# The order of scores and values inside each burst of split-array matmuls

## The chip, the cores and the metric

One core of one Trainium2 chip runs the whole kernel. The metric is the device time of one execution in microseconds (us); the time before is a median of three runs.

## The reference, cut to what matters

```python
def attention(x, context):            # x: 64 x 128 x 256, context: 64 x 128 x 192
    q = (x @ w_q)                      # 16 heads of 64
    k = (context @ w_k)
    v = (context @ w_v)
    attn = softmax(q @ k.T * 64 ** -0.5)
    return (attn @ v) @ w_o + b_o

x = x + attention(layernorm(x), ctx)
h = layernorm(x)
gates = softmax(h @ gate), top 2 of 8 experts, divided by their sum
x = x + sum(gate_e * (relu(h @ W1_e + b1_e) @ W2_e + b2_e))
```

Everything is float32. The kernel keeps the precision of the large products by splitting an operand in a high and a low part (`_h`, `_l`) and adding three products.

## The kernel before, in words

The 8192 tokens are taken as 32 pairs of sequences. The first stage (attention and routing) is one pipeline over the pairs, `iterations`: iteration -1 to 31 and an epilogue, of which 2 to 30 are one hardware loop. The second stage runs tiles of 256 tokens through the experts and is not touched by the change.

Each engine has its own program with the same eight steps n = 0 to 7 in an iteration, written out by hand; the engines meet at semaphores. One iteration handles eight units of attention, u0 to u7. A unit is four heads of one sequence: one bank of scores, 128 queries by 4 x 128 keys.

The steps of TensorE (`body` in the tensor block) are these.

- `scores(it, n)`, at even n, makes the scores of the units n and n+1 at once. A head has 64 channels, so that two heads stand in the two row halves of the array: 8 matmuls of 64 rows and 128 columns, which write `bank_s0` and `bank_s1` in turn (L1422). It may write only when ScalarE has read both banks of the units before: it waits for `s_exp` of unit n-1.
- `transposes` turns the probabilities of the unit two steps before (`LATE`) into `bank_t` (L1411), after GpSimd has normalised them (`s_norm`).
- `product` makes one of the projections that `A_SLOTS` lists for the step: q and k (L1404, L1471, L1472), v (L1479, L1480, L1404), the output o (`three` at L1404), the transposed input t (L1453) and the routing f0.
- `values(it, name, n)`, at the end of odd n, multiplies v with the transposed probabilities of two units: 8 matmuls with all 128 rows and 64 columns, in the two column halves of the array, into `bank_v` (L1437). `VALUES` names them: w3 of the pair before at n = 1, w0, w1 and w2 at n = 3, 5 and 7. It waits for `t_copy` (the transposed probabilities are in SBUF), for `v_lo` (`bank_v` is read out) and for the v product.

So `values` of an odd step and `scores` of the next even step stand next to each other, four times in an iteration. I call the two together a burst, and name it by its even step; 8 matmuls are 16 records in the trace.

The other engines do this with it. VectorE takes the lowest score (`lowest`, L951) when a bank is full. ScalarE takes the exponentials with it (`exps`, L777, four heads, with a record of READ_ACCUMULATOR behind each), copies the transposed probabilities (`copy_t`, L770), the q, k and t products (`hi_part`, L787 to L792) and the context (L828), and reads `bank_v` first (`hi_out`, L807). VectorE reads `bank_v` behind it (`low_out`, L1004), copies v (L969), subtracts the high part of the context (L1157) and makes the routing. GpSimd normalises (`norm`, L669) and sends rows by an indirect DMA (`send`, L662). Every engine works its own list strictly in the order written; ScalarE's list has `hi_out` at the end of an odd step, before `copy_t` and `exps` of the next even step.

The waits at the head of the two functions, and the last lines of `body`:

```python
def scores(it, n):
    ...
    wait(pe, a_hi, it if g else it - 1, "q11" if g else "k01")
    wait(pe, s_exp, it, f"u{n + 1}", 2)
...
def values(it, name, n):
    ...
    wait(pe, a_done, it if name == "w2" else it - 1, f"v{g}{b}")
    wait(pe, t_copy, it, LATE[n][0])
    wait(pe, v_lo, it, LAST[n - 1][0])
...
        if n in VALUES and has(it, VALUES[n][1]):
            values(it, VALUES[n][0], n)
```

Of the kernel before, what the change touches and what calls it, by code (L numbers as in the profile page):

```python
# [62 lines left out]
def wait(engine, signal, it, name, back=0):  # L63

    value = signal.at(it, name)
    if isinstance(value, int):
        value -= back
        if value > 0:
            engine.wait_ge(signal.sem, value)
    else:  # L70
        engine.wait_ge(signal.sem, value - back)


def program(nc, x, ctx, w_all, w_ot, b_o, b_oc, gate, gate_t, w12, b1, b2, out):
# [5 lines left out]
    PAIRS = tokens // (2 * P)  # L80
# [68 lines left out]
    VALUES = {1: ("w3", PREV), 3: ("w0", CUR), 5: ("w1", CUR), 7: ("w2", CUR)}  # L149
# [3 lines left out]
    with ex:  # L153
        def sem(name):
            return ex.enter_context(nc.semaphore(name))
# [29 lines left out]
        made = sem("made")  # L185
        with ExitStack() as a:
# [165 lines left out]
            def has(it, of):  # L352
                first, last = {PREV: (1, PAIRS), CUR: (0, PAIRS - 1), NEXT: (-1, PAIRS - 2), BOTH: (-1, PAIRS),
                               FROM0: (0, PAIRS)}[of]
                return not isinstance(it, int) or first <= it <= last
# [1044 lines left out]
            def _(pe):  # L1400
# [6 lines left out]
                def transposes(it, name, n):  # L1407
                    wait(pe, s_norm, it - 1 if n >= 6 else it, name)
                    wait(pe, t_copy, it, name, 1)
                    for h in range(4):  # L1410
                        last = pe.transpose(bank_t[:, h * P:(h + 1) * P], prob[:, n % 4, h, :], ident[:, :])  # L1411
                    last.then_inc(t_full.sem, 1)

                def scores(it, n):

                    g, b = n // 4, (n % 4) // 2
                    wait(pe, a_hi, it if g else it - 1, "q11" if g else "k01")
                    wait(pe, s_exp, it, f"u{n + 1}", 2)
                    for c in range(CHUNKS // 2):
                        for side in range(2):  # L1420
                            part = slice(side * HEAD, (side + 1) * HEAD)
                            last = pe.matmul(bank_s[side][:, c * P:(c + 1) * P], qt[part, g, c, b * P:(b + 1) * P],  # L1422
                                             kt[part, g, b, c, :], start=True, stop=True, skip_group_check=True)
                            if c == CHUNKS // 2 - 1:
                                last.then_inc(s_full.sem, 1)

                def values(it, name, n):
                    g, b = int(name[1]) // 2, int(name[1]) % 2
# [5 lines that stand above are left out]
                    for head in range(HALF):  # L1434
                        unit, h = head % 2, head // 2
                        side = slice(unit * HEAD, (unit + 1) * HEAD)
                        last = pe.matmul(bank_v[side, h * P:(h + 1) * P],  # L1437
                                         vv[:, g, b, head * HEAD:(head + 1) * HEAD], probt[:, unit, h, :],
                                         start=True, stop=True, skip_group_check=True)
                    last.then_inc(v_full.sem, 1)  # L1440
# [95 lines left out]
                def body(it):  # L1536
                    for n in range(8):

                        if isinstance(it, int) and it == -1 and n == 5:
                            pe.wait_ge(w_lo, Q_READY)  # L1540
                        if isinstance(it, int) and it == 1 and n == 0:
                            pe.wait_ge(w_lo, NW)
                            pe.wait_ge(gate_made, 5)
                        late, of = LATE[n]
                        if n % 2 == 0 and has(it, CUR):
                            scores(it, n)
                        if has(it, of):
                            transposes(it, late, (n - 2) % 8)
                        slots = A_SLOTS_LAST if isinstance(it, int) and it == PAIRS - 1 else A_SLOTS
                        for name, o in slots[n]:  # L1550
                            if has(it, o):
                                if isinstance(it, int) and it == -1 and name == "k00":
                                    pe.wait_ge(w_lo, K_READY)
                                if isinstance(it, int) and it == -1 and name == "v00":
                                    pe.wait_ge(w_lo, V_READY)
                                product(it, name)
                                if isinstance(it, int) and it == -1 and name == "t0":
                                    bias_scores()
                                    keep_busy(8)
                        if n in VALUES and has(it, VALUES[n][1]):  # L1560
                            values(it, VALUES[n][0], n)

                def keep_busy(many):

                    for _ in range(many):
                        pe.matmul(bank_s[0][:, 0:P], prob[:, 0, 0, :], prob[:, 0, 0, :], start=True, stop=True,
                                  skip_group_check=True)
# [10 lines left out]
                def bias_scores():  # L1578

                    pe.wait_ge(gate_made, 2)  # L1580
                    for c in range(DC):
                        last = pe.matmul(bank_v[:, E:2 * E], bo_col[:, c:c + 1].to_broadcast([P, P]), gate_c[:, c, :],
                                         start=c == 0, stop=c == DC - 1, skip_group_check=True)
                    last.then_inc(gate_mean, 1)

                gate_means()
                keep_busy(3)
                pe.wait_ge(made, 20)
                iterations(pe, body)

                def turn_x(j, u):
# [116 lines left out]
```

## Time and profile before

| | |
|---|---|
| median of 3 runs | 1581.21 us (1580.75 to 1581.81) |
| the profiled execution, its own time | 1580.22 us |
| its span in the trace | 1578.5 us |
| TensorE, matmul | 1553.8 us busy, 98% |
| TensorE, weight loads | 1454.0 us busy, 92% |
| VectorE | 1176.1 us busy, 75% |
| ScalarE | 1108.0 us busy, 70% |
| GpSimd | 818.1 us busy, 52% |
| mean granted TensorE clock | 0.994 of full speed |

The profiled execution takes 1.7 us more than its span, which lies around the traced instructions, and is 1.0 us below the median. In the stretch from 95 to 1109 us, which is the looped part of the first stage, TensorE is busy 1011.46 of 1014 us at granted clock 1.00. The busy share counts a matmul from its start to its modelled end, and matmuls overlap; how long a piece of work holds the engine is read from the starts of it and of what follows.

### The profile page before, as it was taken

Reading aid. Unit: us, or ns where it says so; the run is one execution under the profiler, and the core shown is the slowest. Engines: PE = TensorE matmul, PEld = TensorE weight load, DVE = VectorE, ACT = ScalarE, POOL = GpSimd, SP = SyncE. Lnnn points to the kernel's source line nnn. Section 1 sums busy time; section 2 is a strip of 40 time slices with the busy share of each in tenths; the row PEclk is TensorE's granted clock in tenths of the full one; section 3 lists DMA queues with packets and bytes.
Section 4 is the critical chain, followed back from the end, with each engine's and each line's share of the span. In section 5 each row is a group of like instructions: output and inputs, shape, how many; then the busy total and the mean of one; then the engine's idle time right before and its main releaser. Section 6 shows DMA issues by size and latency. Waiting matters only on the chain.

```text
span 1578.5 us, 45424 instructions
## 1 busy us (share of the span) xinstructions
PE 1553.8 (98%) x14150; PEld 1454.0 (92%) x14151; DVE 1176.1 (75%) x3796; ACT 1108.0 (70%) x3357; POOL 818.1 (52%) x946
## 2 busy tenths in 40 slices
PE   8999999999999999999999999999999999999997
PEld 7899999999899999999999989998899999999997
DVE  4777777777777777777777777777788777777775
ACT  5677677677776777767767777676666676777774
POOL 2344545545554554554555455455456555555556
PEclk9999999999999999999999999999999999999999
DMA  6522111222111221211122211122799755555554
GB/s 201 145 72 74 60 60 60 77 90 72 62 60 60 67 94 66 74 60 60 63 75 89 74 60 60 60 67 81 241 231 249 144 86 85 89 86 90 84 84 61
DMA packets 105643, 145.05 MB, mean 92 GB/s; under 512 B 12736, under 2 KB 87616, under 8 KB 105344
## 3 DMA queue, kind: packets, MB, share of 16 engines
q1 hardware_dynamic: 60144, 89.00, 17.8%
q0 software_dynamic: 26816, 37.32, 13.7%
q10 hardware_dynamic: 18640, 18.19, 4.4%
q8 instruction: 23, 0.38, 0.1%
q14 instruction: 20, 0.16, 0.0%
HBM read 77.09 MB, written 67.38 MB: 92 GB/s over the span
## 4 chain that ended last, share of the span: by engine, by line
issue 47%; POOL 22%; PE 9%; DVE 7%; DMA 6%; DVEq 3%; ACT 2%; POOLq 2%; ACTq 1%; SPq 0%
POOL lists L662 7%; DMA out<-stage_room,number 6%; PE bank_a L1404 4%; POOL prob L669 3%; DVE hid L1332 3%; POOL rstd L648 2%; DVE stage_room L1349 2%; POOL stage_room L711 2%; POOL stage_room L707 2%; POOL out L735 2%; DVEq L1344 1%; PE bank_v L1437 1%; POOLq L729 1%; PE bank_s L1422 1%; DVEq L1323 1%
## 5 line engine op out<-in xcount | busy, mean ns | idle before, releaser
L669 POOL TENSOR_TENSOR prob<-prob,inv 128x512 f32<-128x512 f32 x256 | 271.4, 1060 | 520.3 <-DVE inv L956 519.6
L777 ACT ACTIVATE prob<-bank_s,low 128x128 f32<-128x128 f32 x1024 | 363.3, 376 | 40.9 <-DVE low L951 40.9
L735 POOL DMA_INDIRECT out<-stage_room,number x142 | 231.8, 1632 | 53.9 <-issue 53.1
L951 DVE TENSOR_REDUCE low<-bank_s 128x4 f32<-128x512 f32 x256 | 175.4, 685 | 98.0 <-PE bank_s L1422 97.9
L777 ACT ACTIVATION_READ_ACCUMULATOR prob<-bank_s,low 128x1 f32 x1024 | 221.1, 216 | 0.0
L770 ACT ACTIVATE probt<-bank_t 128x512 f32<-128x512 f32 x256 | 153.4, 599 | 89.6 <-PE bank_t L1411 89.6
L1050 DVE SCALAR_TENSOR_TENSOR stage_room<-xin,wo_t 128x256 f32<-128x256 f32 x480 | 178.8, 426 | 0.0
L807 ACT ACTIVATE ot_h<-bank_v 128x512 fp32r<-128x512 f32 x128 | 77.4, 604 | 138.4 <-PE bank_v L1437 138.4
L885 ACT ACTIVATE hidt_h<-hid 128x512 fp32r<-128x512 f32 x142 | 89.7, 632 | 117.4 <-DVE hid L1332 112.2
L1411 PE MATMUL bank_t<-ident,prob 128*128 128x128 f32 x1024 | 161.9, 281 | 4.0 <-POOL prob L669 4.0
L1404 PE MATMUL bank_a<-xt_l,wq_h 128*128 128x256 f32 x512 | 152.4, 298 | 0.3 <-DVE xt_l L966 0.3
L1422 PE MATMUL bank_s<-kt,qt 64*128 64x128 f32 x2048 | 149.7, 286 | 2.3 <-ACT prob L777 2.3
L1422 PEld LDWEIGHTS bank_s<-kt,qt 64*128 64x128 f32 x2048 | 125.1, 188 | 24.6 <-issue 24.4
L662 POOL DMA_INDIRECT lists<-rows,slot x128 | 129.0, 1008 | 33.8 <-issue 33.8
L1404 PE MATMUL bank_a<-wo_l,ot_h 128*128 128x264 f32 x496 | 146.1, 295 | 0.0
L1404 PE MATMUL bank_a<-xt_h,wq_h 128*128 128x256 f32 x512 | 144.5, 282 | 0.0
L1404 PE MATMUL bank_a<-xt_h,wq_l 128*128 128x256 f32 x512 | 144.4, 282 | 0.0
L865 ACT ACTIVATE wst<-homes 128x2048 fp32r x71 | 136.2, 1918 | 9.2 <-issue 9.0
L1437 PE MATMUL bank_v<-probt,vv 128*64 128x128 f32 x2048 | 140.9, 280 | 0.7 <-DVE ot_l L1004 0.4
L1404 PE MATMUL bank_a<-wo_h,ot_l 128*128 128x264 f32 x496 | 141.0, 284 | 0.0
L1404 PE MATMUL bank_a<-wo_h,ot_h 128*128 128x264 f32 x496 | 140.7, 284 | 0.0
L1411 PEld LDWEIGHTS bank_t<-ident,prob 128*128 128x128 f32 x1024 | 114.1, 141 | 25.3 <-POOL prob L669 5.9
(231 smaller groups left out, 4728.9 us busy)
## 6 DMA issues: line engine op xcount, KB each, us to landing
stage_room<-lists ACTq DMA_DIRECT2D x67, 265.0 KB
halves<-stage_room SPq DMA_DIRECT2D x32, 512.0 KB
homes<-halves SPq DMA_DIRECT2D x16, 1024.0 KB, 6.4
xin<-in_x SPq DMA_DIRECT2D x32, 256.0 KB, 2.8
stage_room<-in_x SPq DMA_DIRECT2D x32, 256.0 KB
stage_room<-in_w SPq DMA_DIRECT2D x32, 256.0 KB, 4.3
out<-stage_room SPq DMA_DIRECT2D x32, 256.0 KB, 2.2
cin<-in_ctx SPq DMA_DIRECT2D x32, 128.0 KB, 2.6
```

Of the source, the lines that this page charges most:

```text
L662: pool.indirect_dma_start(lists, bass.IndirectOffsetOnAxis(ap=slot[:, b, k:k + 1], axis=0), rows[:, b, :], None).then_inc(sent, 16)
L669: pool.tensor_tensor(prob[:, n % 4, :, :], prob[:, n % 4, :, :], wide(inv[:, n % 4, :], P), ALU.mult).then_inc(s_norm.sem, 1)
L735: pool.indirect_dma_start(out, bass.IndirectOffsetOnAxis(ap=number[:, u, b:b + 1], axis=0), ysum[:, u, b, :], None, compute_op=ALU.add).th ...
L770: act.activation(probt[:, n % 2, :, :], bank_t[:, :].rearrange("p (h q) -> p h q", h=4), ACT.Copy).then_inc(t_copy.sem, 1)
L777: e = act.activation(prob[:, n % 4, h, :], bank_s[n % 2][:, h * P:(h + 1) * P], ACT.Exp, bias=low[:, n % 4, h:h + 1], scale=-1.0, accum_ou ...
L865: act.activation(wst[u % 2][:, :, :, :], homes[:, bass.ds(e, 2 * DC * H)].rearrange("p (c s h) -> p c s h", c=DC, s=2), ACT.Copy)
L951: dve.tensor_reduce(low[:, n % 4, :], bank_s[n % 2][:, :].rearrange("p (h k) -> p h k", h=4), AX.X, ALU.min).then_inc(s_low.sem, 1)
L1050: last = dve.scalar_tensor_tensor(junk[:, k % 11, :], xin[:, b, :], 1.0, gate_b[:, e, :], ALU.mult, ALU.mult, accum_out=x_two[:, b, e:e + 1])
L1404: last = pe.matmul(dst, stat[s], move[r], start=start and m == 0, stop=stop and m == 2)
L1411: last = pe.transpose(bank_t[:, h * P:(h + 1) * P], prob[:, n % 4, h, :], ident[:, :])
L1422: last = pe.matmul(bank_s[side][:, c * P:(c + 1) * P], qt[part, g, c, b * P:(b + 1) * P], kt[part, g, b, c, :], start=True, stop=True, ski ...
L1437: last = pe.matmul(bank_v[side, h * P:(h + 1) * P], vv[:, g, b, head * HEAD:(head + 1) * HEAD], probt[:, unit, h, :], start=True, stop=Tru ...
```

## The change

`values` is no longer called at the end of its odd step, but in the even step behind it, after that step's `scores` and before its `transposes`; at n = 0 it is the w2 of the iteration before. Only at the end of the last iteration is w2 still called in its own step, since no scores follow there. Nothing else moves, on no engine.

```diff
@@ -1544,6 +1544,11 @@
                         late, of = LATE[n]
                         if n % 2 == 0 and has(it, CUR):
                             scores(it, n)
+                        if (n - 1) % 8 in VALUES:
+                            name, made = VALUES[(n - 1) % 8]
+                            values_of = it - 1 if n == 0 else it
+                            if has(values_of, made):
+                                values(values_of, name, (n - 1) % 8)
                         if has(it, of):
                             transposes(it, late, (n - 2) % 8)
                         slots = A_SLOTS_LAST if isinstance(it, int) and it == PAIRS - 1 else A_SLOTS
@@ -1557,7 +1562,7 @@
                                 if isinstance(it, int) and it == -1 and name == "t0":
                                     bias_scores()
                                     keep_busy(8)
-                        if n in VALUES and has(it, VALUES[n][1]):
+                        if isinstance(it, int) and (it, n) == (PAIRS - 1, 7):
                             values(it, VALUES[n][0], n)
```

TensorE's list in the hardware loop at burst 6, before. `bank_v` is written by the values (`probt` are the transposed probabilities, `vv` is v), `bank_s` by the scores; a row of REGISTER_ALU is the sequencer's arithmetic for a semaphore value.

```order
L1404 MATMUL bank_a<-xt_h,wk_h 128x256
L71 REGISTER_ALU [waits t_copy,a_done]
L1437 MATMUL bank_v<-probt,vv 64x128 [waits v_lo]
L1437 MATMUL bank_v<-probt,vv 64x128 x7
L1422 MATMUL bank_s<-kt,qt 128x128 [waits s_exp,a_hi]
L1422 MATMUL bank_s<-kt,qt 128x128 x7
L1411 MATMUL bank_t<-ident,prob 128x128 [waits t_copy,s_norm]
L1411 MATMUL bank_t<-ident,prob 128x128 x3
```

The same place in the changed kernel:

```order
L1404 MATMUL bank_a<-xt_h,wk_h 128x256
L1422 MATMUL bank_s<-kt,qt 128x128 [waits s_exp,a_hi]
L1422 MATMUL bank_s<-kt,qt 128x128 x7
L71 REGISTER_ALU [waits t_copy,a_done]
L1437 MATMUL bank_v<-probt,vv 64x128 [waits v_lo]
L1437 MATMUL bank_v<-probt,vv 64x128 x7
L1411 MATMUL bank_t<-ident,prob 128x128 [waits t_copy,s_norm]
L1411 MATMUL bank_t<-ident,prob 128x128 x3
```

The wait for `s_exp` now stands ahead of both groups, where only the scores were behind it before; the transposes are behind both groups in either order.

At the top of the loop, burst 0, the values stood at the end of the loop's body, before its branch, and the list began with the scores:

```order
L348 ISA
L71 REGISTER_ALU [waits a_hi]
L1422 MATMUL bank_s<-kt,qt 128x128 [waits s_exp]
L1422 MATMUL bank_s<-kt,qt 128x128 x7
L71 ISA
L71 REGISTER_ALU [waits s_norm]
L1411 MATMUL bank_t<-ident,prob 128x128 [waits t_copy]
```

and now the values follow them there:

```order
L348 ISA
L71 REGISTER_ALU [waits a_hi]
L1422 MATMUL bank_s<-kt,qt 128x128 [waits s_exp]
L1422 MATMUL bank_s<-kt,qt 128x128 x7
L71 ISA
L71 REGISTER_ALU [waits a_done]
L71 ISA [waits t_copy]
L1437 MATMUL bank_v<-probt,vv 64x128 [waits v_lo]
L1437 MATMUL bank_v<-probt,vv 64x128 x7
L71 REGISTER_ALU [waits s_norm]
L1411 MATMUL bank_t<-ident,prob 128x128 [waits t_copy]
```

The values have crossed the loop's branch, and one more row of the sequencer stands in the burst.

## Rows read from the trace of the kernel before

**Rows 1.** Busy time by stretch, the looped part (PE, PEld, DVE, ACT, POOL, clock)

```profile
95.00:1109.00 1014.00, 1011.46 (x9603) 922.86 (x9603) 764.53 (x2770) 724.51 (x2639) 522.41 (x651) 1.00 0.21 69
```

**Rows 2.** Timeline of PE, one loop iteration's bursts 0, 2 and 6 (start, us, instruction)

```profile
500.69 1.09 PE L1437 MATMUL bank_v<-probt,vv 128*64 128x128 f32 x16
...
509.38 1.09 PE L1437 MATMUL bank_v<-probt,vv 128*64 128x128 f32 x16
...
523.19 0.40 PE L1404 MATMUL bank_a<-wv_h,xt_h 128*128 128x512 f32 x1
...
526.58 1.09 PE L1437 MATMUL bank_v<-probt,vv 128*64 128x128 f32 x16
527.60 1.16 PE L1422 MATMUL bank_s<-kt,qt 64*128 64x128 f32 x16
528.69 0.66 PE L1411 MATMUL bank_t<-ident,prob 128*128 128x128 f32 x4
...
534.53 0.39 PE L1404 MATMUL bank_a<-wv_h,xt_h 128*128 128x512 f32 x1
534.85 1.09 PE L1437 MATMUL bank_v<-probt,vv 128*64 128x128 f32 x16
```

**Rows 3.** Timeline of ACT, the same iteration

```profile
501.83 0.60 ACT L807 ACTIVATE ot_h<-bank_v 128x512 fp32r<-128x512 f32 x1 [1.19 <-PE bank_v L1437]
...
508.39 0.23 ACT L777 ACTIVATION_READ_ACCUMULATOR prob<-bank_s,low 128x1 f32 x1
...
523.70 0.63 ACT L828 ACTIVATE xt_h<-cin 128x512 fp32r<-128x512 f32 x1 [0.40 <-PE bank_a L1404]
...
525.70 0.37 ACT L777 ACTIVATE prob<-bank_s,low 128x128 f32<-128x128 f32 x1 [0.87 <-DVE low L951]
...
526.99 0.21 ACT L777 ACTIVATION_READ_ACCUMULATOR prob<-bank_s,low 128x1 f32 x1
...
529.38 0.60 ACT L770 ACTIVATE probt<-bank_t 128x512 f32<-128x512 f32 x1 [0.20 <-PE bank_t L1411]
...
534.53 0.27 ACT L777 ACTIVATION_READ_ACCUMULATOR prob<-bank_s,low 128x1 f32 x1
```

**Rows 4.** Timeline of DVE, the same iteration

```profile
523.62 0.69 DVE L969 COPY vv<-bank_a 128x512 f32<-128x512 f32 x1 [0.23 <-PE bank_a L1404]
...
524.98 0.68 DVE L951 TENSOR_REDUCE low<-bank_s 128x4 f32<-128x512 f32 x1
```

**Rows 5.** Timeline of PE, scores that had no values ahead (iteration 0)

```profile
22.09 0.39 PE L1404 MATMUL bank_a<-wv_h,xt_h 128*128 128x512 f32 x1
22.41 1.16 PE L1422 MATMUL bank_s<-kt,qt 64*128 64x128 f32 x16
...
28.57 1.16 PE L1422 MATMUL bank_s<-kt,qt 64*128 64x128 f32 x16 [2.18 <-ACT prob L777]
```

**Rows 6.** Timeline of ACT, what those scores waited for

```profile
28.21 0.22 ACT L777 ACTIVATION_READ_ACCUMULATOR prob<-bank_s,low 128x1 f32 x1
```

**Rows 7.** Instructions of bank_s: durations in ns, min/median/max

```profile
L1422 PE MATMUL bank_s<-kt,qt x2048: 272/272/580, 22.4 to 1108.0; 64*128 64x128 f32 x187
```

**Rows 8.** Timeline of PE, values that had no scores behind (epilogue)

```profile
1120.56 1.09 PE L1437 MATMUL bank_v<-probt,vv 128*64 128x128 f32 x16 [0.36 <-issue]
1121.59 0.66 PE L1607 MATMUL bank_a<-ident,stage_room 128*128 128x128 f32 x4
```

**Rows 9.** Timelines of PE and of ACT, burst 6 of iteration 30

```profile
1073.99 1.09 PE L1437 MATMUL bank_v<-probt,vv 128*64 128x128 f32 x16
...
1074.41 0.21 ACT L777 ACTIVATION_READ_ACCUMULATOR prob<-bank_s,low 128x1 f32 x1
```

**Rows 10.** Timeline of PE, transposes that waited (iteration 31)

```profile
1104.14 0.66 PE L1411 MATMUL bank_t<-ident,prob 128*128 128x128 f32 x4 [1.73 <-POOL prob L669]
```

**Rows 11.** Timelines of ACT and of POOL around burst 4 of the same iteration

```profile
518.90 0.98 POOL L662 DMA_INDIRECT lists<-rows,slot  x1 [0.30 <-issue]
...
520.51 0.60 ACT L807 ACTIVATE ot_h<-bank_v 128x512 fp32r<-128x512 f32 x1 [1.30 <-PE bank_v L1437]
```

## The prediction

> **What bounds the kernel.** I read the busy time by stretch first. In the looped part of the first stage TensorE is busy 1011.46 of 1014 us at granted clock 1.00, VectorE 764, ScalarE 725, GpSimd 522 [rows 1]: TensorE sets the pace, and only its own list can change the time. Next I read TensorE's timeline over one iteration. Burst 0 begins at 500.69 and again at 534.85 [rows 2]: 34.16 us for an iteration, with no wait for another engine in it. So the question is what the swap does to (a) the time that a burst holds TensorE and (b) the waits at its head. For (b) I read, at each burst, when ScalarE finished the exponentials that the scores wait for.
>
> **(a) The switches of the array.** The matmuls are the same, and so are their number and sizes; what changes is who stands next to whom.
> Product to values takes 0.32 us from start to start (534.53 to 534.85) [rows 2]; product to scores, in iteration 0 with no values ahead, also 0.32 (22.09 to 22.41) [rows 5].
> Values to scores takes 1.02 (526.58 to 527.60) [rows 2]; values to transposes, in the epilogue, 1.03 (1120.56 to 1121.59) [rows 8].
> Scores to transposes takes 1.09 (527.60 to 528.69) [rows 2].
> Two of the three new neighbours are therefore in the trace, at the old price. Scores to values is not. The nearest row is scores to transposes, 1.09, which also goes from row halves to all rows, and I take that: a burst costs 0.32 + 1.09 + 1.02 in either order, a difference of 0.
> The bounds: a record of the scores lasts 0.272 [rows 7], so 16 of them that span 1.16 start every (1.16 - 0.27) / 15 = 0.059 us, the last at 0.89, and 0.20 passes from it to the next instruction. If that switch cost nothing, it would be 0.14 less; if it cost one such loss more, 0.14 more. There are 126 bursts with both parts (2 in iteration 0, 4 in each of 1 to 31), so this term lies between -18 and +18 us.
> No row shows this switch, and there the Trainium skill has a rule, in TensorEngine Tiling (Array Packing), Key Properties: a change of tiling mode drains the engine. A burst has three such changes in both orders, so by that page too the term is 0.
> The further row of the sequencer in burst 0 I cost at nothing: such rows stand in front of the scores there already, and TensorE has a matmul in flight over them. The branch is now between a product and the scores; between values and scores it lost nothing visible.
>
> **(b) The waits at the head of a burst.** The scores of burst n may start once the exponentials of unit n-1 are done. Behind the last exponential's record there is a hand-over: in iteration 0 the record ended at 28.43 [rows 6] and the scores that waited for it started at 28.57 [rows 5], 0.14 later.
> Burst 6: the values start at 526.58 [rows 2], but the exponentials of u5 end at 526.99 + 0.21 = 527.20 [rows 3]. Until now the values ran under that and the scores at 527.60 found all ready. Now the scores come first and cannot start before 527.34: **a wait of 0.76 us.**
> Do these exponentials come earlier in the changed kernel? They start at 525.70 after ScalarE sat idle 0.87 for the lowest scores of u5 [rows 3]. VectorE makes those from 524.98, behind the copy of v at 523.62, for which it sat idle 0.23 until TensorE's product [rows 4], whose last matmul started at 523.19 [rows 2]. From 523.62 on VectorE's three instructions are back to back. The chain is hung on a product of TensorE that keeps its distance from burst 6, and the scores of burst 4, though 1.02 earlier, don't shorten it. I take the wait whole.
> It is so in every iteration from 0 to 28 and in 30: there the values start at 1073.99 and the record ends at 1074.62 [rows 9], 0.63 later, as at 526.58 and 527.20 (in the first two within 0.1 of it). In 29 GpSimd was late with the transposes just before, and the exponentials were done in time. 30 x 0.76 = 22.8.
> Burst 0: the exponentials of u7 end at 534.53 + 0.27 = 534.80 [rows 3] and the burst begins at 534.85 [rows 2], so the scores would wait until 534.94: 0.09. ScalarE is busy without a gap from its copy at 529.38 [rows 3], which comes after the transposes of burst 6; the wait there moves both by the same amount, so the 0.09 stays. 30 such bursts (iterations 2 to 31): 2.7.
> Burst 2: the exponentials are done at 508.39 + 0.23 = 508.62 [rows 3] and the burst begins at 509.38 [rows 2], 0.76 later and more than 0.14; burst 4 is alike. Nothing.
> In the last iteration the transposes of u3 wait 1.73 for GpSimd [rows 10], behind scores that now come 1.02 earlier; but the scores of burst 6, which wait there already, now hold the values and transposes back by about 1.0. I take 0, between -1 and +1.
>
> That the wait costs all of its length rests on TensorE's list being worked in order. The row shows it: scores that waited 2.18 in iteration 0 left the engine idle, with transposes and products behind them [rows 5]. The Trainium skill says the same in TensorE: Matmul & The Clock Gate, on which tiles overlap: weight loads may be pulled ahead, matmuls start and end in strict order. By the page the sum is mine; if the values, ready all the time, could pass the waiting scores, their 1.02 would cover the 0.76 and the sum would be about 0.
>
> **What moves and costs nothing.** The lowest scores can be taken 1.02 earlier at each burst, which gives VectorE and GpSimd slack that TensorE doesn't wait for. `bank_v` is full 1.09 later. ScalarE reads it 1.14 after the values start (501.83) [rows 3], now at 500.69 + 1.09 + 1.14 = 502.92, and is done at 503.5. ScalarE's idle time (1.19 at this read) ahead of this read covers the shift; if it were gone, the copy of the transposed probabilities would be late, and the exponentials after it. No DMA and no queue is passed by anything moved.
>
> **The sum.** 0 + 22.8 + 2.7 = +25.5 us. The profiled execution took 1580.22, so 1605.7 for it; it lies 1.0 below the median, and the median should become **1606.7 us**. An iteration should take 34.16 + 0.85 = 35.0. A measurement of this kernel can tell about 0.2% (3.2 us) from no change.
>
> **The rivals.**
> *Not slower.* The burst's own time shrinks by more than the waits: the scores' successor costs less when it is the values. Per iteration 0.85 of waits has to be won in 4 bursts, 0.21 each; that is the point from which it decides. The 0.14 lost after the scores isn't enough (25.5 - 18 = +7.5, 1589); with a third of the entry's 0.32 (0.10) won too it would be 25.5 - 126 x 0.24 = -4.7, 1576.5. For it: the one switch that no row shows. Against: the entry and the exit are in the trace, at the old price. 4% for faster, 4% for about no change; in the latter I also put that TensorE passes the waiting scores by (1581).
> *The switch costs more.* Another 0.14 at each of 126 bursts: +18, 1624. 5%.
> *ScalarE slips at burst 4.* There it reads `bank_v` at 520.51 [rows 11], not 1.14 after the values' start at 518.50 but 0.87 later, in each of the iterations 2 to 28 and 30, those in which GpSimd's last indirect DMA starts at 518.90 [rows 11]. If that delay is tied to the DMA's time, it is over when the read is now due (518.50 + 1.09 + 1.14 = 520.73), and nothing happens. If it goes with the read, that comes at 521.60, 1.09 late; some 0.20 of idle time before the copy (as at 529.38) and 0.40 before the context's copy [rows 3] take 0.60 of it, and 0.49 reaches the exponentials of u5 and the wait at burst 6: 28 x 0.49 = +14, 1620. The same distance to the DMA in all these iterations speaks for the first. 13%.
> *The wait at burst 6 is shorter,* since VectorE runs ahead somewhere that I don't see: half of it gives 1595. 6%.
>
> **How the numbers follow.** The forecast, 1606.7, has 68%, with a few us either way for the hand-over and the last iteration. The range takes in the forecast with a mixture of the halved wait or a cheaper switch below, and the slip above: 1597 to 1620; outside lie the cases of no loss and the dearer switch. Faster 4%, same 4%, slower 92%.
>
> **What would show it.** In the changed profile the scores should wait for ScalarE's exponentials some 60 times, 30 of them about 0.7 us, at burst 6 and burst 0 only; an iteration should be 35.0 us; scores to values should be 1.09 and values to transposes 1.03; ScalarE's wait for `bank_v` should grow and VectorE's for `bank_s` fall. I am wrong on (a) if the distance from scores to values isn't 1.09, and on (b) if the exponentials of u5 end earlier against the last matmul of the product of v than the 4.01 us of here (from 523.19 to 527.20).

## The result, and the profile after

The changed kernel takes **1604.05 us** (median of 4 runs, 1602.72 to 1605.78), the kernel before 1581.51 on the same chip (4 runs, 1580.75 to 1581.89). The ratio is 1.0142, 95% interval 1.0127 to 1.0157: slower by 22.5 us. Forecast were 1606.7 and +25.5. The profiled execution of after took 1605.78 (span 1604.0), 25.6 more than the profiled one of before.

TensorE's share of the span falls from 98 to 97%. Its busy time grows from 1553.8 to 1557.5 us, so that 21.8 of the 25.5 us by which the span grew are idle time. The page of after, in its part on busy time, in the group of the scores (after "|" busy time and mean ns; then the idle time before them and what ended most of it), and in the chain:

```profile
PE 1557.5 (97%) x14150; PEld 1457.4 (91%) x14151; DVE 1175.8 (73%) x3796; ACT 1105.0 (69%) x3357; POOL 809.2 (50%) x946
...
PE 83%; ACT 4%; DVE 4%; issue 3%; DMA 2%; POOL 1%; DVEq 1%; ACTq 0%; SPq 0%; POOLq 0%
...
L1422 PE MATMUL bank_s<-kt,qt 64*128 64x128 f32 x2048 | 148.7, 284 | 24.7 <-ACT prob L777 24.6
```

The list of waits of after (total us, times, longest). The last line is the new one:

```profile
ACT ot_h L807 <- PE bank_v L1437: 245.9, 127, 3.2
...
DVE low L951 <- PE bank_s L1422: 37.2, 65, 3.5
ACT prob L777 <- DVE low L951: 33.6, 34, 4.4
...
PE bank_s L1422 <- ACT prob L777: 24.6, 32, 2.2
```

The same lines of before: 

```profile
ACT ot_h L807 <- PE bank_v L1437: 138.4, 95, 2.4
DVE low L951 <- PE bank_s L1422: 97.9, 126, 4.1
ACT prob L777 <- DVE low L951: 40.9, 65, 4.4
...
PE bank_s L1422 <- ACT prob L777: 2.3, 2, 2.2
```

TensorE waited 2.3 us for exponentials before and waits 24.6 now, in 32 places instead of 2. ScalarE waits longer for `bank_v`, which is full later; VectorE waits less for `bank_s`, which is full earlier. Both signs are as forecast.

Where those waits stand shows in TensorE's timeline of after, over one iteration (bursts 6 and 0, then 4, for [rows 2]):

```profile
502.64 0.39 PE L1404 MATMUL bank_a<-wv_h,xt_h 128*128 128x512 f32 x1
...
505.81 0.28 PE L1404 MATMUL bank_a<-xt_h,wk_h 128*128 128x256 f32 x1
506.79 1.16 PE L1422 MATMUL bank_s<-kt,qt 64*128 64x128 f32 x16 [0.70 <-ACT prob L777]
507.88 1.09 PE L1437 MATMUL bank_v<-probt,vv 128*64 128x128 f32 x16
508.91 0.66 PE L1411 MATMUL bank_t<-ident,prob 128*128 128x128 f32 x4
...
514.75 0.39 PE L1404 MATMUL bank_a<-wv_h,xt_h 128*128 128x512 f32 x1
515.07 1.16 PE L1422 MATMUL bank_s<-kt,qt 64*128 64x128 f32 x16
516.16 1.09 PE L1437 MATMUL bank_v<-probt,vv 128*64 128x128 f32 x16
517.19 0.66 PE L1411 MATMUL bank_t<-ident,prob 128*128 128x128 f32 x4
...
532.88 1.16 PE L1422 MATMUL bank_s<-kt,qt 64*128 64x128 f32 x16
533.98 1.09 PE L1437 MATMUL bank_v<-probt,vv 128*64 128x128 f32 x16
```

Only burst 6 waits, 0.70 us; its scores are 0.77 late, since the last product's modelled end reaches 0.07 further into the wait, and these 0.07 count as busy. Burst 0 starts 0.32 after the last product's start, without a wait. Scores to values is 1.09 and values to transposes 1.03. The next burst 0 begins at 550.00: an iteration takes 34.93 us, not 34.16.

ScalarE's timeline of after at the same two places (for [rows 3]):

```profile
505.14 0.37 ACT L777 ACTIVATE prob<-bank_s,low 128x128 f32<-128x128 f32 x1 [0.87 <-DVE low L951]
...
506.44 0.21 ACT L777 ACTIVATION_READ_ACCUMULATOR prob<-bank_s,low 128x1 f32 x1
...
514.75 0.27 ACT L777 ACTIVATION_READ_ACCUMULATOR prob<-bank_s,low 128x1 f32 x1
```

The exponentials of u5 end at 506.44 + 0.21 = 506.65 and the scores that waited start at 506.79, 0.14 later, the hand-over of [rows 5, 6]. ScalarE has waited 0.87 for the lowest scores, exactly as before [rows 3], and from the last matmul of the product of v (502.64) to the end of the exponentials are 4.01 us, as many as before: the chain did not move against TensorE's products.

### The profile page after: what moved, and what is told of

It is laid out like the page before. It is cut to its first block, busy times and chain, and to the rows that moved or that the text cites. A ratio compares the mean times of both kernels' runs of the same rounds, so it can differ in the third digit from the quotient of the medians.

```text
span 1604.0 us, 45424 instructions
## 1 busy us (share of the span) xinstructions
PE 1557.5 (97%) x14150; PEld 1457.4 (91%) x14151; DVE 1175.8 (73%) x3796; ACT 1105.0 (69%) x3357; POOL 809.2 (50%) x946
## 4 chain that ended last, share of the span: by engine, by line
PE 83%; ACT 4%; DVE 4%; issue 3%; DMA 2%; POOL 1%; DVEq 1%; ACTq 0%; SPq 0%; POOLq 0%
PE bank_a L1404 35%; PE bank_s L1422 9%; PE bank_v L1437 8%; PE bank_t L1411 7%; PE bank_t L1404 5%; PE bank_v L1404 5%; PE bank_s L1404 5%; ACT prob L777 2%; PE bank_a L1479 2%; PE bank_a L1480 2%; PE bank_a L1471 1%; PE bank_a L1472 1%; PE bank_a L1612 1%; DMA out<-stage_room,number 1%; DVE low L951 1%
## 5 line engine op out<-in xcount | busy, mean ns | idle before, releaser
L777 ACT ACTIVATE prob<-bank_s,low 128x128 f32<-128x128 f32 x1024 | 363.3, 378 | 33.6 <-DVE low L951 33.6
L1050 DVE SCALAR_TENSOR_TENSOR stage_room<-xin,wo_t 128x256 f32<-128x256 f32 x480 | 174.4, 418 | 0.0
L1422 PE MATMUL bank_s<-kt,qt 64*128 64x128 f32 x2048 | 148.7, 284 | 24.7 <-ACT prob L777 24.6
```

The costliest lines, as they stand in the source:

```text
L777: e = act.activation(prob[:, n % 4, h, :], bank_s[n % 2][:, h * P:(h + 1) * P], ACT.Exp, bias=low[:, n % 4, h:h + 1], scale=-1.0, accum_ou ...
L1050: last = dve.scalar_tensor_tensor(junk[:, k % 11, :], xin[:, b, :], 1.0, gate_b[:, e, :], ALU.mult, ALU.mult, accum_out=x_two[:, b, e:e + 1])
```

## The experiments

The theory was that the whole loss is one wait per iteration, of burst 6 for the exponentials of u5, and that the new neighbours on the array cost nothing. The rivals were a dearer or cheaper switch, paid at all bursts, and a slip of ScalarE. All kernels below compute everything that the reference does. Ratios are taken against the kernel before on the same chip: 1580.63 (27 runs, 1578.27 to 1582.58) for e1 to e4, and 1579.37 (17 runs, 1577.16 to 1582.4) for e5 to e7.

### One burst of four, and the other three

In `e1_burst6_only` the scores go first at burst 6 alone; `e2_bursts_0_2_4` is its complement. Against the changed kernel (of e2 the set is `(0, 2, 4)` in both lines):

```diff
-                        if (n - 1) % 8 in VALUES:
+                        if (n - 1) % 8 in VALUES and n in (6,):
...
-                        if isinstance(it, int) and (it, n) == (PAIRS - 1, 7):
+                        own = (n + 1) % 8 not in (6,) or (isinstance(it, int) and (it, n) == (PAIRS - 1, 7))
+                        if n in VALUES and has(it, VALUES[n][1]) and own:
```

> Scores first at burst 6 alone; bursts 0, 2 and 4 as in the kernel before. Theory A (the loss is the wait of the scores of burst 6 for the exponentials of u5, the order itself costs nothing): 0.77 us in each of iterations 0 to 30, some 1604, and TensorE's wait for ScalarE's exponentials about 0.70 us, 29 to 31 times. Rival B (scores to values is a dearer switch and costs its share at each burst): a quarter of the loss, some 1587. Rival C (the later reading of bank_v at bursts 0, 2 and 4 holds back ScalarE): the wait would be shorter here than in the changed kernel and the time below 1600. Beside it: ScalarE's reading of bank_v at burst 4 should again be late, about 2.0 us after the start of the values instead of 1.14, in iterations 2 to 30; if so, an exponential of u4 and all behind it are as before.

> Scores first at bursts 0, 2 and 4, values first at burst 6. Theory A: no wait for exponentials in the loop, 34.16 us for an iteration, 1581 to 1583 in all; what is left is iteration 0, where ScalarE reads bank_v 1 us later in front of the copy of w_o, and the transposes of u3 wait 1 us or more longer for GpSimd. Rival B (dearer switch): three quarters of the loss, some 1598. The hand-over at burst 0 that the prediction put at 0.09 us each should not show: at most 0.03.

e1: 1602.94 us (4 runs, 1601.81 to 1604.63), ratio 1.0141 [1.0126, 1.0157]: the whole loss, from a quarter of the edit. e2: 1582.31 (11 runs, 1580.26 to 1583.5), ratio 1.0011 [1.0001, 1.0020], within what I called no change: three quarters of the edit, 94 of the 126 new neighbours, cost at most 3.2 us. In the lists of waits, first of e1, then of e2:

```profile
PE bank_s L1422 <- ACT prob L777: 23.6, 31, 2.2
```

```profile
PE bank_s L1422 <- ACT prob L777: 2.5, 2, 2.2
```

An iteration of e1 takes 34.93 us, one of e2 34.16. A switch priced at 126 bursts is out, in either direction, and so is a wait at burst 0: e2 has scores first there, and none waits.

### The exponentials made earlier

If burst 6 waits because u5's exponentials are late, VectorE can mend it: `e3_after_early_lowest` is the changed kernel with the lowest scores of u5 taken behind the copy of `v10`, ahead of the context's low part and the copy of `v11` (not in the last iteration). `e4_before_early_lowest` makes the same edit in the kernel before, as a control.

```diff
-                        if has(it, CUR):
+                        last = isinstance(it, int) and it == PAIRS - 1
+                        if has(it, CUR) and (n != 5 or last):
                             lowest(it, n)
...
                         for name, of in slots[n][1:]:
-                            outcome(it, made_in, name, of)
+                            if name != "v11" or last:
+                                outcome(it, made_in, name, of)
+                        if n == 4 and has(it, CUR) and not last:
+                            lowest(it, 5)
...
+                        if n == 4 and not last:
+                            outcome(it, made_in, "v11", CUR)
```

> The changed kernel, with the lowest scores of u5 taken by VectorE right behind the copy of the v product v10, in front of the context's low part and of the copy of v11 (which it now follows). Theory A: the exponentials of u5 start at ScalarE's own pace behind its copy, about 0.9 us earlier against the product of v11, and end 0.2 us before burst 6: the wait of 0.70 goes away entirely, 34.16 us for an iteration, 1581 to 1584 in all. If the chain behind the wait is another one (ScalarE's copies rather than VectorE's list), the wait stays at 0.4 or more and the time above 1594. Rival B: no change against the changed kernel, 1604.

> The kernel before with the same move on VectorE's list as in the run above, and values first everywhere. Control: no wait of TensorE is taken away by it, so 1581.5 within 1.5 us. If it were faster, a gain in the run above would not belong to the wait alone; if it were slower, the low part of the context or the copy of v11 holds TensorE, at the k product of step 5 or at the values.

e3: 1582.52 us (11 runs, 1579.84 to 1584.43), ratio 1.0010 [1.0001, 1.0019]: the changed order, at all four bursts, without its loss. e4: 1580.93 (11 runs), ratio 1.0001 [0.9992, 1.0010]: the edit by itself gives nothing. The list of waits of e3 (lines moved by 6: L1428 are the scores):

```profile
ACT prob L777 <- DVE low L951: 6.7, 3, 4.4
PE bank_s L1428 <- ACT prob L777: 3.7, 2, 2.2
```

ScalarE's wait for the lowest scores went from 33.6 us in 34 places to 6.7 in 3, and TensorE's from 24.6 to 3.7. An iteration takes 34.16 again. The wait at burst 6 is the loss, all but 1.9 us of it; the order as such, at 126 bursts, costs no more than that.

### The rest of 1.7 to 1.9 us: iteration 0

e2 and e3 have no wait at burst 6 and are still 1.7 and 1.9 above the kernel before. Their traces differ from it in iteration 0, where `prepare` makes `w_o`'s high part on ScalarE (L765) and low part on VectorE (L941) behind the read of `bank_v` at burst 4. `e5_024_not_first` is e2 with that one burst in the old order:

```diff
-                        if (n - 1) % 8 in VALUES and n in (0, 2, 4):
+                        if (n - 1) % 8 in VALUES and n in (0, 2, 4) and not (isinstance(it, int) and (it, n) == (0, 4)):
...
-                        own = (n + 1) % 8 not in (0, 2, 4) or (isinstance(it, int) and (it, n) == (PAIRS - 1, 7))
+                        own = (n + 1) % 8 not in (0, 2, 4) or (isinstance(it, int) and (it, n) in ((PAIRS - 1, 7), (0, 3)))
```

> Scores first at bursts 0, 2 and 4, values first at burst 6 and at burst 4 of iteration 0. The theory on what remained of the loss (1.7 us with bursts 0, 2 and 4, 1.9 us with the early lowest scores): in iteration 0 ScalarE reads bank_v ahead of its copy of w_o, which the scores' reduction on VectorE waits for, so that scores first at this one burst costs 1.1 us. Then the wait of the transposes of u3 in iteration 0 goes from 2.96 back to 1.9 or less, and the time to 1580.6 to 1581.6. Rival: the remainder lies in the last iteration, or is not there; then that wait is shorter and the time stays 1.7 above the kernel before.

1579.13 us (12 runs, 1576.1 to 1580.93), ratio 0.9997 [0.9989, 1.0006]: no rest is left to be seen. TensorE's timeline of e5, the transposes of u3 in iteration 0; in after they wait 2.96 there, before 0.45:

```profile
46.57 0.65 PE L1411 MATMUL bank_t<-ident,prob 128*128 128x128 f32 x4 [1.18 <-POOL prob L669]
```

Iteration 0 is also where TensorE's clock differs from one execution to the next, so single waits there are rough. That the order matters there rests on the medians of e2 and e5, each against its own kernel before: +1.7 and -0.2. These intervals overlap a little, so the term, 1.9 us by the medians, is barely clear of the noise, and its size is not well known.

### What a change of the array's division costs

The prediction had no row for a division change by itself. `e6_before_halves` cuts each burst of the kernel before into half of the values, half of the scores, and the other halves: the same matmuls, two more changes per burst.

```diff
                         if n % 2 == 0 and has(it, CUR):
-                            scores(it, n)
+                            before_it = it - 1 if n == 0 else it
+                            name, made = VALUES[(n - 1) % 8]
+                            if has(before_it, made):
+                                scores(it, n, (0, 1))
+                                values(before_it, name, (n - 1) % 8, range(4, 8))
+                                scores(it, n, (2, 3))
+                            else:
+                                scores(it, n)
...
                         if n in VALUES and has(it, VALUES[n][1]):
-                            values(it, VALUES[n][0], n)
+                            alone = isinstance(it, int) and (it, n) == (PAIRS - 1, 7)
+                            values(it, VALUES[n][0], n, range(8) if alone else range(4))
```

> The order before, with each burst cut in four: half of the values, half of the scores, the other half of the values, the other half of the scores. The matmuls are the same; a burst has two changes of the array's division more. By the rows of the kernel before (0.20 us from the last scores to what follows, 0.22 from the last values, against 0.055 inside) each costs about 0.15: 126 bursts x 0.30 = 38, with some 0.2 us of wait at burst 6 about 1622. Rival: the 0.15 is lost only when the work that follows is of all rows and all columns, and a change between the two divisions is cheap: below 1600.

1631.14 us (4 runs, 1628.65 to 1633.01), ratio 1.0320 [1.0305, 1.0335]: +51.8. TensorE's timeline of e6, a burst 2 and the burst 6 of one iteration:

```profile
535.66 0.66 PE L1437 MATMUL bank_v<-probt,vv 128*64 128x128 f32 x8
536.25 0.72 PE L1423 MATMUL bank_s<-kt,qt 64*128 64x128 f32 x8
536.89 0.66 PE L1437 MATMUL bank_v<-probt,vv 128*64 128x128 f32 x8
537.48 0.71 PE L1423 MATMUL bank_s<-kt,qt 64*128 64x128 f32 x8
538.13 0.66 PE L1411 MATMUL bank_t<-ident,prob 128*128 128x128 f32 x4
...
553.57 0.66 PE L1437 MATMUL bank_v<-probt,vv 128*64 128x128 f32 x8
554.34 0.71 PE L1423 MATMUL bank_s<-kt,qt 64*128 64x128 f32 x8
554.99 0.66 PE L1437 MATMUL bank_v<-probt,vv 128*64 128x128 f32 x8
555.57 0.71 PE L1423 MATMUL bank_s<-kt,qt 64*128 64x128 f32 x8
556.22 0.66 PE L1411 MATMUL bank_t<-ident,prob 128*128 128x128 f32 x4
```

Eight values take 0.59 to the scores where sixteen take 1.02 [rows 2]: a matmul is (1.02 - 0.59) / 8 = 0.054, and 0.59 - 8 x 0.054 = 0.16 is the change. Eight scores take 0.64 to the values where sixteen take 1.09: 0.056 each, and 0.19 for the change. The plain burst lasts 2.47 instead of 2.11 from its first values to the transposes. The second burst lasts 2.65: with half of the values the scores start only 0.59 behind, and u5's exponentials aren't done, so they start 0.18 later still. 96 x 0.36 + 30 x 0.54 = 50.8 of the 51.8. I had expected some 42, with 0.30 for the two changes and the wait at burst 6 counted in; the two changes at 0.36 are 126 x 0.06 = 7.6 of the difference.

The Trainium skill says in TensorEngine Tiling (Array Packing), Key Properties, that a change of tiling mode drains the engine. The trace agrees in so far as each added change costs TensorE time, 0.16 to 0.19 us in this kernel; that this time is a drain no run here shows.

### The late read of `bank_v` at burst 4

`e7_before_late_send` is the kernel before with GpSimd's sends one step later (one run with a profile):

```diff
-                        if n in (1, 2) and has(it - 1, PREV):
-                            send(it - 1, n - 1)
+                        if n in (2, 3) and has(it - 1, PREV):
+                            send(it - 1, n - 2)
```

> The kernel before with GpSimd's four indirect DMAs sent one step later (behind the normalising of u2 and u3). It asks where the 0.87 us come from by which ScalarE reads bank_v late at burst 4. If they belong to an indirect DMA that starts 0.4 us after the values, the read is now 1.14 behind the start of the values, as at the other bursts, and another read may be late in its place. If they belong to SyncE's transfers at that place or to ScalarE's own list, it stays at 2.0. The time should be within 5 us of the kernel before, and may be above, since GpSimd comes later to the normalising of u4.

It took 1583.32 us (one run). Its timelines of TensorE (values of burst 4), of ScalarE and of GpSimd, one fence each:

```profile
519.16 1.09 PE L1437 MATMUL bank_v<-probt,vv 128*64 128x128 f32 x16
```

```profile
520.30 0.60 ACT L807 ACTIVATE ot_h<-bank_v 128x512 fp32r<-128x512 f32 x1 [0.44 <-PE bank_v L1437]
```

```profile
518.29 1.05 POOL L662 DMA_INDIRECT lists<-rows,slot  x1 [0.17 <-issue]
519.65 0.98 POOL L662 DMA_INDIRECT lists<-rows,slot  x1 [0.30 <-issue]
```

The read comes 1.14 after the values' start, not 2.01 as in [rows 11]. So the late read goes with when GpSimd sends, and not with the read. But in e7 too one indirect DMA starts 0.87 us before the values, where it is 0.90 in the kernel before, and another 0.49 behind their start, where it is 0.40 in the kernel before: the distance to these DMAs alone doesn't say why one read is late and the other isn't. That stays open.

## Why the prediction was right, and where it wasn't

**(a) The switches: 0 forecast, 0 found.** Scores to values is 1.09, the value taken from scores to transposes. e2, with three bursts of four in the new order, is within 0.2% of before, and e3 with all four too. Since a change costs 0.16 to 0.19 in either direction (e6), a reordering that keeps three changes per burst keeps their cost. The choice of the nearest row was right, and the bounds of 18 us were wider than needed.

**(b) Burst 6: 22.8 forecast, about 23 found.** An iteration is 34.93 - 34.16 = 0.77 longer, against 0.76, and 30 of them give 23.1. e1 shows that this burst carries it, and e3 that u5's exponentials are its cause. The step to the wait's whole length, that nothing passes the waiting scores on TensorE, held: the values, ready all the time, stood behind them. By the Trainium skill, TensorE: Matmul & The Clock Gate, Part 3, The mechanism, matmuls start and end in strict order; the trace agrees, with the ready values 1.09 behind the scores that waited 0.70 (506.79 and 507.88). The iterations are 1 to 30, not 0 to 28 and 30: in 0 TensorE was held up earlier in the iteration, so that the exponentials were done 0.74 before, and in 29 the transposes no longer wait for GpSimd's late send, behind scores that come 1.02 earlier, so burst 6 waits there as elsewhere.

**Burst 0: 2.7 forecast, 0.1 found.** Here a term was mis-sized: the hand-over. I took 0.14 from the end of ScalarE's last record to the scores, measured at [rows 5, 6], and put it at every burst. Timelines of after, of ScalarE and then of TensorE's weight loads (PEld), at burst 0 of iteration 31:

```profile
1108.61 0.27 ACT L777 ACTIVATION_READ_ACCUMULATOR prob<-bank_s,low 128x1 f32 x1
```

```profile
1109.00 1.00 PEld L1422 LDWEIGHTS bank_s<-kt,qt 64*128 64x128 f32 x16 [0.42 <-issue]
```

And at burst 0 of the iteration shown in the result, where the record of ScalarE begins at 514.75 and ends at 515.02:

```profile
515.07 0.97 PEld L1422 LDWEIGHTS bank_s<-kt,qt 64*128 64x128 f32 x16 [0.35 <-ACT prob L777]
```

In iteration 31 the scores start at 1109.03, 0.14 behind the record's end, and 0.09 late against the last product: this is the term as forecast, once. In the loop, behind a record of the same length, they start at 515.07, only 0.05 behind its end, and that is just when the product lets them start anyway. The two differ in how they wait. At burst 6 of the loop, at burst 0 of iteration 31 and at [rows 5] the wait for the exponentials has a row of TensorE's sequencer of its own ahead of the weight load: at burst 6 of after this row starts 0.04 behind the record's end, the weight load 0.11 behind it and the scores 0.14. At burst 0 of the loop the wait for the exponentials is the weight load's own, with no such row before it; that this makes the difference no run isolates. So the waits are 32, not some 60, and the iteration is 34.93, not 35.0.

**"What moves and costs nothing" was wrong once.** I covered the later read of `bank_v` with ScalarE's idle time, and said what would be late if it were gone. In iteration 0 it is: behind that read stands the copy of `w_o`, and behind that VectorE's low part and the lowest scores of u3. ScalarE's timeline of iteration 0, first before, then after:

```profile
38.55 0.60 ACT L807 ACTIVATE ot_h<-bank_v 128x512 fp32r<-128x512 f32 x1 [0.56 <-PE bank_v L1437]
39.05 1.99 ACT L765 ACTIVATE wo_h<-raw_o 128x1024 fp32r<-128x1024 f32 x2
```

```profile
41.55 0.60 ACT L807 ACTIVATE ot_h<-bank_v 128x512 fp32r<-128x512 f32 x1 [1.53 <-PE bank_v L1437]
42.05 2.00 ACT L765 ACTIVATE wo_h<-raw_o 128x1024 fp32r<-128x1024 f32 x2
```

The pair is 3.0 later, of which 2.0 is TensorE's own lateness by then (its granted clock was 0.90 on average from 22 to 39 us, in before 1.00 from 22 to 37) and about 1 the swap. It reaches TensorE before the transposes of u3, which start 5.80 behind the read in before (44.35), after (47.35), e2 and e5 alike; they wait 2.96 in after, and 1.18 in e5, with the values first again (this burst at a granted clock of 0.54, from 38.75 to 42.45). Everywhere else the cover held.

**The last iteration: 0 forecast, -1.0 found.** At its burst 0 the profiled executions stand 26.76 apart, in the epilogue, where [rows 8] are, 25.77. The transposes of u3 wait 0.78, by now for ScalarE's copy, instead of 1.73 for GpSimd [rows 10], and what follows absorbs the wait of 1.50 at burst 6. That is the lower bound that I had given, but some 0.5 of it belongs to the clock: in before the granted clock was 0.55 from 1113 to 1116, in after 1.00 at the same place (1139 to 1142).

**The sum.** Of the 25.6 between the profiled executions, 2.0 lie before burst 4 of iteration 0 (clock and start-up), 2.4 in the rest of that iteration, 22.4 from there to the last iteration (30 waits of 0.77, less 0.86 that the late send of iteration 29 had cost before), and -1.0 and -0.2 behind. Of the 2.4, 1.0 is the swap and 1.4 the clock again: from the transposes of u3 to burst 6 TensorE takes 4.68 us in after, at a granted clock of 0.65 (47.35 to 52.03), and 3.29 in before, at 1.00 (44.35 to 47.64). So the agreement of the profiled pair with +25.5 is luck: the 2.0 and the 1.4 are not the change's, and they stand in for the 2.7 that burst 0 does not cost. Without these clock terms the same count gives 22.4 + 1.0 - 0.5 - 0.2 = 22.7, and the medians gave 22.5.

**The rivals.** A slip of ScalarE at burst 4 was priced at +14. In after the read comes 1.14 after the values' start at every burst of the loop, 4 as well (533.98 to 535.12): no slip. e1, with values first at burst 4, has it late again by 0.82. A cheaper or dearer switch is refuted by e2, and a shorter wait at burst 6 by the wait itself, 0.65 to 0.71 in 29 of 30 iterations.

## What to carry to other kernels

On an engine that works its list in order, put the group whose input arrives last at the end of a burst: work that is ready costs nothing there and covers the wait, and behind the waiting group it covers nothing. To price such a swap, take for each group the time at which its last input is done against the burst's start; the work's own cost cancelled here, where the number of changes of the array's division stayed. Then look at the iterations that aren't like the others, where an engine's idle time, the cover in the loop, is filled with preparation.

## What the runs showed that I had not expected

A change between the row halves of the scores and the column halves of the values cost 0.16 to 0.19 us in either direction (e6), with three of them in a burst of 2.11 us. Before the runs the nearest row was the 0.20 after the scores, and it could have been anything from nothing to twice that in the other direction.

ScalarE's read of a full `bank_v` came 0.81 to 0.92 us late in the same place (burst 4 of before, e1 and e4) of nearly every iteration, with TensorE's matmuls and its own earlier work done, and was on time when the read or GpSimd's sends were moved (after, e2, e7). It cost nothing here, and its mechanism isn't known.

The hand-over from ScalarE's last record to the waiting scores was 0.14 us where the wait had a row of TensorE's sequencer of its own, and 0.05 where the weight load carried it (burst 0 of the loop, in after, e2 and e3).
